# A fused attention and feed-forward kernel: the stretch from y to the gated tiles in a new order

## The chip, the cores and the metric

The kernel runs on one core of one Trainium2 chip. The metric is device time in microseconds (us) of one launch, the median of several runs.

## The reference, cut to what matters

Four batches of 256 tokens of width 128 (float32) go through four blocks, each with a residual. The stretch in question is the end of the first block and the second.

```python
# block 1 (x is normed first; emb = norm(x) + ctx)
y  = sigmoid(q) * num / den                      # AFT attention, then y @ wo + bo
a  = layer_norm(y @ wo + bo + emb) * gamma + beta
ff = relu(a @ w1 + b1) @ w2 + b2                 # 128 -> 512 -> 128
x  = x + (layer_norm(ff + a) * gamma + beta)
# block 2, on norm(x), BitLinear: rows quantised to 8 bits, weights to -1, 0, 1
gate = silu(bitlinear(norm(x), w_gate))          # 128 -> 512
up   = bitlinear(norm(x), w_up)
x    = x + bitlinear(gate * up, w_down)          # rows of gate*up quantised again
# block 3: 16-head attention over ctx (keys, values from ctx, masked), block 4: 8-expert top-1 FFN
```

## The kernel before

All instructions of an engine stand in one list written out by hand; there is no planner. Engines meet at counting semaphores (`sig[...]`), and each list is run strictly in order, so an instruction that waits holds everything behind it. A batch b has two row tiles of 128 tokens (t = 0, 1) and owns two PSUM banks, `bank(b, 0)` and `bank(b, 1)`. Matmuls in near-float32 are made of three float16 passes over high and low parts: ScalarE writes the high part (a rounded copy), VectorE or GpSimd the low part (source minus high).

The stages around the change, for b = 0 to 3 each:

- GpSimd multiplies `th` and `rden` to y (L419); TensorE turns y (L1261 is its transpose helper, L1252 its matmul helper); ScalarE and VectorE write its high and low columns `colsY` (L610, L816); TensorE multiplies by wo.
- Norm LN_A: VectorE takes statistics and moments (L798, L804), GpSimd adds epsilon (L377) and raises to -0.5 (L380) in `rstd_of`, VectorE writes normed rows (L811), TensorE turns them, ScalarE applies gamma and beta (L622, L623), VectorE writes the low part (L816, `n_mem`).
- First layer (TensorE, 4 blocks of 128 hidden columns a batch), relu on ScalarE (L631, high part) and VectorE (L966, low part), second layer on TensorE. A batch order is kept: all four first layers, then all four second layers, with the mask's column counts (L962, and `count_mm`) after the second of these.
- Output norm LN_OUT in pairs of batches: statistics from PSUM, centring with gamma (L980), root on GpSimd, residual into x1 (L987), which adds `xb`, the block's input plus beta, made by GpSimd in eight additions (L431). Then the norm LN_FFN of x1: statistics, root, and on GpSimd the negated mean (L376) and the shift `nmr` (L386); ScalarE writes the rows (L616).
- Row maxima (L1013) and scales (L1006, L1009) on VectorE, one common factor `fac` for all batches (L1020), rounding on ScalarE (L662), turning on TensorE, columns qT on ScalarE (L675).
- Gate and up products for the eight tiles of `GU_ORDER`, (0,0) (1,0) (0,1) (1,1) (2,0) ... (3,1): TensorE, silu on ScalarE (L686), product with up on VectorE (L1033), its maximum (L1027), and per batch a scale again (L1006, L1009). GpSimd (L468) and ScalarE (L679) round the gated tiles for the down product.

Between these stand pieces for later blocks: on GpSimd the low parts of the weights (L392), scaling and rounding of the quantised weights (L425, L438), the low part of the transposed ctx (L441), and after the first `gscale` two clearings (L450, L452) and the residual mask (L457, L462); on ScalarE the high parts (L559), the ctx copy (L627), the column mask (L639 to L643), the value copy `va` (L654) and key copies (L649); on VectorE the small biases `kb16` (L945) and `mbias16` (L949), clipping of the quantised weights (L957) and low parts of keys (L999); on TensorE the projections of values and of half the keys, between the second layers and the turned quantised rows. SP loads everything at the start, except the mask, which waits for the low parts of w1 and w2 and lands in their float32 place.

## Time and profile before

| | us |
|---|---|
| median of 3 runs (lowest, highest) | 248.2 (247.9, 248.48) |
| the profiled execution, its own time | 249.16 |
| its span, first to last instruction | 247.3 |
| busy: TensorE, VectorE, ScalarE, GpSimd | 192.6, 173.2, 135.4, 119.1 |
| mean granted TensorE clock, share of full speed | 0.952 |

The engines are called PE (TensorE; PEld is its weight load), DVE (VectorE), ACT (ScalarE), POOL (GpSimd) and SP. Times are counted from the start of the span. Busy shares are averages over all stages; what bounds a stage is read from the chain of waits and the idle times in it. A row that covers several instructions gives the time from the first's start to the last's end; an instruction's own span overlaps the next one's start by 0.05 to 0.1 us on VectorE and ScalarE, so the distance between two starts is the better price where a queue is full.

### The profile page before, as it was taken

The page shows a single profiled execution, that of the slowest core. Times are in us where ns is not written, and L with a number is a line of the kernel's source. Part 1 is how long each engine was busy: PE and PEld are TensorE (multiplying, and loading weights), DVE is VectorE, ACT ScalarE, POOL GpSimd, SP SyncE. Part 2 cuts the span into 40 slices and gives each one's busy share as a digit, 9 for nine tenths or more (in the row PEclk, how much of TensorE's full clock was granted, in tenths as well). Part 3 has the DMA queues.
Part 4 walks back from the last instruction along what each step waited for, and adds up shares of the span by engine and source line. Part 5 has one row for each costly group of instructions (what it writes and reads, how often), then busy time and mean ns, then how long its engine had stood idle before and what let it go on. Part 6 is the DMA issues. An engine that isn't in the chain of part 4 may idle for free.

```text
span 247.3 us, 4771 instructions
## 1 busy us (share of the span) xinstructions
PE 192.6 (78%) x1750; PEld 134.4 (54%) x1750; DVE 173.2 (70%) x454; ACT 135.4 (55%) x271; POOL 119.1 (48%) x231
## 2 busy tenths in 40 slices
PE   0479865998328479776989988988897895999994
PEld 0358653897203177552433543543555784798883
DVE  4678888994684979869767786886755655739252
ACT  2246744939476578435767567667794256260100
POOL 8131768996649857831587784784221022000000
PEclk9999999999955789998899999999999997999999
DMA  5895040000000000000000000000000000000000
GB/s 169 324 398 219 0 170 4 0 4 0 3 1 0 0 0 3 3 3 3 0 0 5 1 0 3 0 3 0 3 1 3 0 0 4 0 3 21 24 21 21
DMA packets 4461, 8.75 MB, mean 35 GB/s; under 512 B 514, under 2 KB 3026, under 8 KB 4052
## 3 DMA queue, kind: packets, MB, share of 16 engines
q1 hardware_dynamic: 3636, 7.78, 8.4%
q10 hardware_dynamic: 800, 0.63, 0.8%
q8 instruction: 16, 0.26, 0.5%
q14 instruction: 9, 0.07, 0.1%
HBM read 7.89 MB, written 0.52 MB: 34 GB/s over the span
## 4 chain that ended last, share of the span: by engine, by line
PE 31%; POOL 29%; DVE 19%; issue 9%; ACT 7%; DMA 2%; SPq 1%; POOLq 0%; DVEq 0%
PE ps L1252 28%; POOL gate_pt L514 6%; POOL rstd L380 5%; POOL w L400 3%; PE ps L1261 3%; POOL x_in L431 3%; DMA wf<-weights_dram 2%; POOL w L392 2%; POOL vareps L377 2%; DVE gate_pt L1033 2%; DVE mx L1090 2%; DVE amax L1027 2%; DVE stats L798 2%; DVE half_c L1080 2%; ACT gate_pt L758 1%
## 5 line engine op out<-in xcount | busy, mean ns | idle before, releaser
L1090 DVE TENSOR_REDUCE mx<-ps 128x2 f32<-128x512 f32 x64 | 42.2, 686 | 16.6 <-PE ps L1252 16.5
L758 ACT ACTIVATE gate_pt<-ps 128x512 f32<-128x512 f32 x64 | 37.2, 603 | 15.6 <-PE ps L1252 15.3
L1252 PE MATMUL ps<-w,hid_xm 128*128 128x256 f16 (+1 forms) x288 | 30.3, 263 | 0.1
L514 POOL TENSOR_SCALAR gate_pt<-ka_mem 32x256 f16<-32x256 f16 x64 | 25.5, 399 | 4.4
L1252 PE MATMUL ps<-gate_pt,half_c 128*128 128x512 f16 x64 | 25.0, 393 | 3.2 <-issue 1.9
L1252 PEld LDWEIGHTS ps<-w,hid_xm 128*128 128x128 f16 x288 | 25.4, 101 | 3.4 <-issue 0.4
L1252 PE MATMUL ps<-qb,gate_pt 128*128 128x256 f16 x128 | 25.4, 281 | 0.8
L1261 PE MATMUL ps<-cst,rows 128*128 128x128 f32 x32 | 7.5, 333 | 18.0 <-ACT rows L662 8.8
L1252 PE MATMUL ps<-gate_pt,hid_xm 128*32 128x256 f32 x256 | 20.4, 390 | 1.5 <-ACT gate_pt L758 1.5
L1252 PEld LDWEIGHTS ps<-qb,gate_pt 128*128 128x128 f16 x128 | 9.5, 99 | 18.7 <-issue 11.4
L380 POOL TENSOR_TENSOR rstd<-vareps,halfs 128x2 f32<-128x2 f32 x24 | 17.7, 738 | 2.0
L501 POOL TENSOR_SCALAR spread<-mx 128x16 f16<-128x16 f32 x32 | 5.9, 201 | 25.0 <-DVE mx L1090 18.7
L1261 PEld LDWEIGHTS ps<-cst,rows 128*128 128x128 f32 x32 | 3.6, 156 | 22.0 <-ACT rows L662 10.1
L376 POOL TENSOR_SCALAR nmean<-moments 128x2 f32<-128x2 f32 x8 | 2.8, 344 | 24.8 <-DVE moments L804 24.7
L377 POOL TENSOR_SCALAR vareps<-moments 128x2 f32<-128x2 f32 x24 | 6.6, 274 | 12.3 <-DVE moments L804 10.8
L1252 PE MATMUL ps<-brow,esel 128*128 128x128 f16 x56 | 11.3, 225 | 0.0
L1252 PE MATMUL ps<-wf,w 128*128 128x256 f16 x96 | 11.1, 272 | 0.0
L1252 PE MATMUL ps<-stage,w 128*128 128x256 f16 x96 | 11.1, 273 | 0.0
L1252 PEld LDWEIGHTS ps<-gate_pt,half_c 128*128 128x128 f16 x64 | 6.4, 100 | 7.7 <-issue 5.5
L747 ACT ACTIVATE half_b<-ps 128x1024 f16<-128x1024 f32 x8 | 8.3, 1040 | 3.8 <-PE ps L1252 3.8
L1261 PE MATMUL ps<-cst,emb 128*128 128x128 f32 x8 | 2.2, 371 | 10.2 <-DVE emb L850 10.2
L1252 PE MATMUL ps<-ffw,qd_mem 128*128 128x512 f16 x16 | 7.1, 599 | 3.9 <-DVE gate_pt L1033 3.9
(221 smaller groups left out, 505.6 us busy)
## 6 DMA issues: line engine op xcount, KB each, us to landing
stage<-weights_dram SPq DMA_DIRECT2D x2, 1024.0 KB, 11.1
wf<-weights_dram SPq DMA_DIRECT2D x4, 256.0 KB, 8.5
wf<-mask_dram SPq DMA_DIRECT2D x1, 1024.0 KB, 4.8
eb_oT<-ffw_dram SPq DMA_DIRECT2D x1, 768.0 KB, 8.2
ctx_in<-ctx_rows_dram ACTq DMA_DIRECT2D x4, 128.0 KB, 5.9
x_in<-x_dram SPq DMA_DIRECT2D x4, 128.0 KB, 3.1
gate_pt<-ctx_cols_dram SPq DMA_DIRECT2D x1, 512.0 KB, 8.5
out_dram<-ctx_in SPq DMA_DIRECT2D x4, 128.0 KB, 1.7
```

Of the source, the lines that this page charges most:

```text
L377: nc.gpsimd.tensor_scalar(vareps[:, ln, b, :], moments[:, ln, b, :, 1], EPS, 1.0, ALU.add, ALU.mult).then_inc(sig["ln_vareps"], 1)
L380: nc.gpsimd.tensor_tensor(rstd[:, ln, b, :], vareps[:, ln, b, :], halfs[:, 0:TILES], ALU.pow).then_inc(sig["ln_rstd"], 1)
L392: nc.gpsimd.tensor_tensor(w16[:, 1, a:z], wf32(name), w16[:, 0, a:z], ALU.subtract)\
L400: nc.gpsimd.tensor_tensor(w16[:, 1, a:z][:, cols], wf32(name)[:, cols], w16[:, 0, a:z][:, cols], ALU.subtract)\
L431: ins = nc.gpsimd.tensor_tensor(xb[:, b, t], x_in[:, b, t], beta_b[:, :], ALU.add)
L501: ins = nc.gpsimd.tensor_scalar(spread[:, n % 2, t].rearrange("p (g r) -> p g r", g=4)[:, :, 28:32], mx[:, b, 4 * quad:4 * quad + 4, t:t + ...
L514: ins = nc.gpsimd.tensor_scalar(kz[part, n % KRING, k], ka[part, b, quad], 1.0, 0.0, ALU.mult, ALU.add)
L747: nc_act(oh[:, b % 2, 4 * half:4 * half + 4].rearrange("p e n -> p (e n)"), pair(ONEHOT_PAIRS[b]).rearrange("p a n -> p (a n)"), ACT.Copy) ...
L758: nc_act(pt[:, head % PRING].rearrange("p t n -> p (t n)"), ps[:, 2 + head % 2, :], ACT.Exp, scale=DK ** -0.5).then_inc(sig["probs"], 1)
L1090: V.tensor_reduce(mx[:, b, head:head + 2, t], score_bank(4 * n + i).rearrange("p (h n) -> p h n", h=2), AX.X, ALU.max).then_inc(sig["smax" ...
L1252: return nc.tensor.matmul(dst, lhsT, rhs, start=start, stop=stop, skip_group_check=True)
L1261: return nc.tensor.transpose(dst, src, ident)
```

## The change

The same arithmetic is done in another order, and some small operations are merged or moved.

- GpSimd: y of batches 0 and 1 ahead of the low part of wo, the others behind it; the roots of LN_A before the low part of w2; roots of batches 2 and 3 of LN_A in one pair of instructions, those of LN_OUT and LN_FFN in one per two batches; negated mean and shift of LN_FFN gone; wq and wo1 behind the ctx part; the eight additions of beta gone.
- ScalarE: y's high parts ahead of the splits of wk, wv, wq, wo1; ctx copy ahead of LN_A's columns; the split of m1 before the last relu; rows, rounding, keys and gates of batches 2 and 3 follow those of 0 and 1.
- VectorE: one addition of beta over all batches and kb16 ahead of y's low parts; the low parts of the hidden tiles, output norms and mask interleaved; the shift of LN_FFN in one instruction per two batches; scales and factors per two batches; the list is written out.
- TensorE: turning, first and second layers interleaved; half the keys of batches 2 and 3 between gate and up products of batches 0 and 1.

The diff, cut to its core (the other hunks rename counts, or turn loops over b into the functions that the lists call):

```diff
+ROOTS = [(LN_IN, (0,)), (LN_IN, (1,)), (LN_IN, (2,)), (LN_IN, (3,)), (LN_A, (0,)), (LN_A, (1,)), (LN_A, (2, 3)),
+         (LN_OUT, (0, 1)), (LN_FFN, (0, 1)), (LN_OUT, (2, 3)), (LN_FFN, (2, 3)),
+         (LN_ATT, (0,)), (LN_ATT, (1,)), (LN_ATT, (2,)), (LN_ATT, (3,)),
+         (LN_MOE, (0,)), (LN_MOE, (1,)), (LN_MOE, (2,)), (LN_MOE, (3,))]
+
+
+def nth_root(ln, b):
+
+    return 1 + [b in bs and of == ln for of, bs in ROOTS].index(True)
+
+
+def nth_shift(ln, b):
+
+    return b // 2 + 1 if ln == LN_FFN else B // 2 + b + 1
+
+
+MAXIMA = ["row 0", "row 1", "gate 0", "row 2", "gate 1", "row 3", "gate 2", "gate 3", "gate 4", "gate 5", "gate 6", "gate 7"]
+
+
...
-            def rstd_of(ln, b):
-
-                pool.wait_ge(sig["ln_moments"], nth_norm(ln, b))
-                if ln in NMR_TURN:
-                    nc.gpsimd.tensor_scalar(nmean[:, ln, b, :], moments[:, ln, b, :, 0], -1.0, 0.0, ALU.mult, ALU.add)
-                nc.gpsimd.tensor_scalar(vareps[:, ln, b, :], moments[:, ln, b, :, 1], EPS, 1.0, ALU.add,
+            def rstd_of(ln, *bs):
+
+                cols = slice(bs[0], bs[-1] + 1)
+                pool.wait_ge(sig["ln_moments"], nth_norm(ln, bs[-1]))
+                if ln == LN_MOE:
+                    nc.gpsimd.tensor_scalar(nmean[:, ln, bs[0], :], moments[:, ln, bs[0], :, 0], -1.0, 0.0, ALU.mult, ALU.add)
+                nc.gpsimd.tensor_scalar(vareps[:, ln, cols, :], moments[:, ln, cols, :, 1], EPS, 1.0, ALU.add,
                                         ALU.mult).then_inc(sig["ln_vareps"], 1)
-                pool.wait_ge(sig["ln_vareps"], nth_norm(ln, b))
-                nc.gpsimd.tensor_tensor(rstd[:, ln, b, :], vareps[:, ln, b, :], halfs[:, 0:TILES],
-                                        ALU.pow).then_inc(sig["ln_rstd"], 1)
+                pool.wait_ge(sig["ln_vareps"], nth_root(ln, bs[0]))
+                nc.gpsimd.tensor_tensor(rstd[:, ln, cols, :].rearrange("p b t -> p (b t)"),
+                                        vareps[:, ln, cols, :].rearrange("p b t -> p (b t)"),
+                                        halfs[:, 0:len(bs) * TILES], ALU.pow).then_inc(sig["ln_rstd"], 1)
...
+            def gated(b):
+                pool.wait_ge(sig["ysig"], b + 1)
+                nc.gpsimd.tensor_tensor(y[:, b], th[:, b], rden[:, b], ALU.mult).then_inc(sig["y"], 1)
+
+            def ffn_weights_scaled(k):
+                return nc.gpsimd.tensor_scalar(ffw_in[:, k], ffw_in[:, k], wscale[:, k:k + 1], MAGIC, ALU.mult, ALU.add)
+
+            gated(0)
+            gated(1)
             a, z = SEG["wo"]
             pool.wait_ge(sig["w_hi"], 2)
             nc.gpsimd.tensor_tensor(w16[:, 1, a:z], wf32("wo"), w16[:, 0, a:z], ALU.subtract).then_inc(sig["w_lo"], 1)
+            gated(2)
+            gated(3)
             split_lo("w1", 3)
+            rstd_of(LN_A, 0)
+            rstd_of(LN_A, 1)
+            rstd_of(LN_A, 2, 3)
             split_lo("w2", 4)
-
-            for b in range(B):
-                pool.wait_ge(sig["ysig"], b + 1)
-                nc.gpsimd.tensor_tensor(y[:, b], th[:, b], rden[:, b], ALU.mult).then_inc(sig["y"], 1)
-            for b in range(B):
-                rstd_of(LN_A, b)
-
             pool.wait_ge(sig["ffscale"], 1)
             for k in range(3):
-                ins = nc.gpsimd.tensor_scalar(ffw_in[:, k], ffw_in[:, k], wscale[:, k:k + 1], MAGIC, ALU.mult, ALU.add)
+                ins = ffn_weights_scaled(k)
             ins.then_inc(sig["ffw_r"], 1)
-            pool.wait_ge(sig["l_gb"], 32)
-            pool.wait_ge(sig["rows_ready"], nth(R_IN, B - 1))
-            for b in range(B):
-                for t in range(TILES):
-                    ins = nc.gpsimd.tensor_tensor(xb[:, b, t], x_in[:, b, t], beta_b[:, :], ALU.add)
-                ins.then_inc(sig["xb"], 1)
             split_lo("wk", 5)
             split_lo("wv", 6)
-            split_lo("wq", 7)
-            split_lo("wo1", 8)
             pool.wait_ge(sig["ffw_c"], 1)
             nc.gpsimd.tensor_scalar(ffw16[:, :, :].rearrange("p k n -> p (k n)"), ffw_in[:, :, :].rearrange("p k n -> p (k n)"),
                                     -MAGIC, 1.0, ALU.add, ALU.mult).then_inc(sig["ffw_ready"], 1)
             pool.wait_ge(sig["ctxT_hi"], 1)
             nc.gpsimd.tensor_tensor(ctxT[:, 1], ctxT_in, ctxT[:, 0], ALU.subtract).then_inc(sig["ctxT_ready"], 1)
+            split_lo("wq", 7)
+            split_lo("wo1", 8)
             for first in range(0, B, 2):
-                for b in (first, first + 1):
-                    rstd_of(LN_OUT, b)
-                for b in (first, first + 1):
-                    rstd_of(LN_FFN, b)
-                    rows_shift(LN_FFN, b)
+                rstd_of(LN_OUT, first, first + 1)
+                rstd_of(LN_FFN, first, first + 1)
...
-            for name in ("w1", "w2", "wk", "wv", "wq", "wo1"):
-                split_hi(name)
+            split_hi("w1")
+            split_hi("w2")
             for b in range(B):
                 act.wait_ge(sig["turned"], nth(T_Y, b))
                 nc_act(colsY[:, 0, b], bank(b, 1)[:, 0:T], ACT.Copy).then_inc(sig["cols_hi"], 1)
 
+            for name in ("wk", "wv", "wq", "wo1"):
+                split_hi(name)
+            act.wait_ge(sig["l_ctxT"], 16)
+            act.wait_ge(sig["attn_mm"], B)
+            nc_act(ctxT[:, 0], ctxT_in, ACT.Copy).then_inc(sig["ctxT_hi"], 1)
...
+            for b in range(B):
+                if b == B - 1:
+                    split_hi("m1")
                 act.wait_ge(sig["hid_mm"], b + 1)
                 nc_act(hid16[:, 0, b], pair(b), ACT.Relu).then_inc(sig["hid_hi"], 1)
...
+            ffn_rows(0)
+            ffn_rows(1)
             for b in range(B):
                 act.wait_ge(sig["vproj"], b + 1)
                 for t in range(TILES):
                     ins = nc_act(va[:, b, t, :, 0:DK],
                                  bank(b, 1)[:, t * D:(t + 1) * D].rearrange("p (h k) -> p h k", h=NH), ACT.Copy)
                 ins.then_inc(sig["va_ready"], 1)
-
-            def round_rows(b):
-
-                act.wait_ge(sig["ascale"], nth(0, b))
-                for t in range(TILES):
-                    ins = nc_act(rows[:, b, t], rows[:, b, t], ACT.Copy, scale=amax[:, b, 1, t:t + 1], bias=MAGIC)
-                ins.then_inc(sig["q1"], 1)
-
-            for b in range(B):
-                act_rows(LN_FFN, b, lambda t: x1[:, b, t])
-                if b == B - 1:
-                    round_rows(0)
-                    round_rows(1)
-                key_hi(b, 0)
+            round_rows(0)
+            round_rows(1)
+            key_hi(0, 0)
+            key_hi(1, 0)
+            quantised_columns(0)
+            quantised_columns(1)
+            gate(0)
+            gate(1)
+            ffn_rows(2)
+            ffn_rows(3)
+            key_hi(2, 0)
+            gate(2)
+            key_hi(3, 0)
+            gate(3)
             round_rows(2)
             round_rows(3)
-            for b in range(B):
-                act.wait_ge(sig["turned"], nth(T_QUANT, b))
-                nc_act(qT[:, b], bank(b, 0)[:, 0:T], ACT.Copy, bias=-MAGIC).then_inc(sig["q1T_ready"], 1)
-
-            def round_gated(b):
-                act.wait_ge(sig["ascale"], nth(1, b))
-                nc_act(g[:, b, 1], g[:, b, 1], ACT.Copy, scale=amax[:, b, 3, 1:2], bias=MAGIC).then_inc(sig["q2_act"], 1)
-
-            for u, (b, t) in enumerate(GU_ORDER):
-                act.wait_ge(sig["gu_mm"], u + 1)
-                act.wait_ge(sig["gscale"], 1)
-                if t:
-                    act.wait_ge(sig["g"], u - 1)
-                nc_act(silu[:, b], bank(b, 0), ACT.Silu, scale=fac[:, b, 0, t:t + 1]).then_inc(sig["silu"], 1)
-                if (b, t) in ((2, 1), (3, 1)):
-
-                    round_gated(b - 2)
+            quantised_columns(2)
+            quantised_columns(3)
+            gate(4)
+            gate(5)
+            gate(6)
+            round_gated(0)
+            gate(7)
+            round_gated(1)
...
+            dve.wait_ge(sig["l_gb"], 32)
+            dve.wait_ge(sig["rows_ready"], nth(R_IN, B - 1))
+            V.tensor_tensor(xb[:, :, :, :].rearrange("p b t n -> p (b t) n"), x_in[:, :, :, :].rearrange("p b t n -> p (b t) n"),
+                            beta_b[:, :].unsqueeze(1).to_broadcast([P, B * TILES, D]), ALU.add).then_inc(sig["xb"], 1)
+            dve.wait_ge(sig["mbias_hi"], 1)
+            V.scalar_tensor_tensor(kb16[0:2, :], kb_h[:, :], c("lo_2", 2), kb_in[:, :], ALU.mult, ALU.add)\
+                .then_inc(sig["mbias_ready"], 1)
...
+            def ffn_shift(first):
+                two = slice(first, first + 2)
+                dve.wait_ge(sig["ln_rstd"], nth_root(LN_FFN, first))
+                V.scalar_tensor_tensor(nmr[:, LN_FFN, two, :], moments[:, LN_FFN, two, :, 0], -1.0, rstd[:, LN_FFN, two, :],
+                                       ALU.mult, ALU.mult).then_inc(sig["ln_nmr"], 1)
...
+            def row_scales(first):
+                two = slice(first, first + 2)
+                quant_scale(two, 0, nth_max("row", first + 1))
+                V.tensor_tensor(fac[:, two, 0:2, :], amax[:, two, 0:1, :].to_broadcast([P, 2, 2, TILES]),
+                                mean[:, 0:2].unsqueeze(1).unsqueeze(3).to_broadcast([P, 2, 2, TILES]), ALU.mult)\
+                    .then_inc(sig["gscale"], 1)
...
+            hidden_lo(0)
+            dve.wait_ge(sig["mbias_hi"], 2)
+            dve.wait_ge(sig["cols_zero"], 2)
+            V.scalar_tensor_tensor(mbias16[0:2 * NE, 0:EH + D], mbias_h[:, :], c("lo_16", 2 * NE), mbias_in[:, :], ALU.mult, ALU.add)\
+                .then_inc(sig["mbias_ready"], 1)
+            hidden_lo(1)
+            dve.wait_ge(sig["y"], B)
+            dve.wait_ge(sig["l_mask"], 16)
+            V.tensor_scalar(ind[:, :, :, :].rearrange("p a t n -> p (a t n)"), mask_in.rearrange("p a t n -> p (a t n)"),
+                            0.0, None, ALU.is_equal).then_inc(sig["mask_ind"], 1)
+            hidden_lo(2)
+            out_stats(0)
+            out_centred(0)
+            hidden_lo(3)
+            out_stats(1)
+            out_centred(1)
+            dve.wait_ge(sig["mbias_ready"], 2)
+            for j in range(2):
+                V.tensor_scalar(out_bias[0:2 * NE, j * D:(j + 1) * D], mbias16[0:2 * NE, EH:EH + D],
+                                c("parity")[0:2 * NE, j:j + 1], None, ALU.mult).then_inc(sig["mbias_ready"], 1)
+            residual(0)
+            residual(1)
+            ffn_stats(0)
+            out_stats(2)
+            out_stats(3)
+            ffn_shift(0)
+            out_centred(2)
+            out_centred(3)
+            residual(2)
+            residual(3)
+            row_max(0)
+            row_max(1)
+            row_scales(0)
+            ffn_stats(2)
+            key_lo(0, 0)
+            key_lo(1, 0)
+            ffn_shift(2)
+            gate_up(0)
+            gate_up(1)
+            gate_max(0)
+            row_max(2)
+            gate_up(2)
+            gate_max(1)
+            row_max(3)
+            row_scales(2)
+            key_lo(2, 0)
+            gate_up(3)
+            gate_max(2)
+            key_lo(3, 0)
+            gate_max(3)
+            gate_scale(0)
+            gate_scale(1)
+            gate_up(4)
+            gate_up(5)
+            gate_max(4)
+            gate_up(6)
+            gate_max(5)
+            gate_up(7)
+            gate_max(6)
+            gate_max(7)
+            gate_scale(2)
+            gate_scale(3)
...
+            normed_turned(0)
+            normed_turned(1)
+            normed_turned(2)
+            pe.wait_ge(sig["w_lo_pool"], 1)
+            first_layer(0)
+            normed_turned(3)
+            first_layer(1)
+            first_layer(2)
+            pe.wait_ge(sig["w_lo_pool"], 2)
+            second_layer(0)
+            first_layer(3)
+            second_layer(1)
+            pe.wait_ge(sig["mask_ind"], 1)
+            for a in range(B):
+                for t in range(TILES):
+                    ins = mm(bank(a // 2, 1)[:, (a % 2) * T:(a % 2 + 1) * T], ones16[:, 0:P], ind[:, a, t], t == 0,
+                             t == TILES - 1)
+            ins.then_inc(sig["count_mm"], 1)
+            second_layer(2)
+            second_layer(3)
...
+            keys_first_half(0)
+            keys_first_half(1)
+            quantised_turned(0)
+            quantised_turned(1)
+            pe.wait_ge(sig["ffw_ready"], 1)
+            gate_up(0)
+            gate_up(1)
+            keys_first_half(2)
+            gate_up(2)
+            keys_first_half(3)
+            gate_up(3)
+            quantised_turned(2)
+            quantised_turned(3)
+            gate_up(4)
+            gate_up(5)
+            gate_up(6)
+            gate_up(7)
...
```

## Rows read from the trace of the kernel before

**Rows 1.** The chain of waits, 30 to 60 us: start, length (us), engine, tile, line.

```profile
41.53 2.66 POOL eb_oT L425 x3
...
44.19 6.44 POOL x_in L431 x8
...
55.08 2.10 POOL y_mem L441
```

**Rows 2.** The waits, 26 to 110 us: who for whom, total us, times, longest.

```profile
ACT rows L616 <- POOL nmr L386: 5.7, 4, 4.0
...
DVE emb L987 <- POOL rstd L380: 5.6, 4, 2.8
```

**Rows 3.** The timeline of VectorE, gate stretch: start, length (us), then the instructions.

```profile
77.19 1.53 DVE L1033 SCALAR_TENSOR_TENSOR gate_pt<-gate_pt,fac,ps 128x512 f32<-128x512 f32 x2 [2.73 <-ACT gate_pt L686]
...
80.45 0.68 DVE L1027 TENSOR_REDUCE amax<-gate_pt 128x1 f32<-128x512 f32 x1
...
81.05 0.74 DVE L1033 SCALAR_TENSOR_TENSOR gate_pt<-gate_pt,fac,ps 128x512 f32<-128x512 f32 x1
...
89.57 0.17 DVE L1009 RECIPROCAL amax<-amax 128x2 f32<-128x2 f32 x1
```

**Rows 4.** The timeline of GpSimd: y, two roots, the mask additions.

```profile
32.37 2.77 POOL L419 TENSOR_TENSOR y<-th,rden 128x256 f32<-128x256 f32 x4
...
37.56 0.70 POOL L380 TENSOR_TENSOR rstd<-vareps,halfs 128x2 f32<-128x2 f32 x1
...
38.62 0.70 POOL L380 TENSOR_TENSOR rstd<-vareps,halfs 128x2 f32<-128x2 f32 x1
...
79.89 4.48 POOL L462 TENSOR_TENSOR wf<-wf,colsA 128x512 bf16<-128x512 bf16 x4
```

**Rows 5.** Instructions grouped by line and shape, GpSimd: count | busy us, mean ns.

```profile
L485 POOL TENSOR_TENSOR wnorm<-wnorm,minus_ones 128x8 f32<-128x8 f32 x1 | 1.7, 1657 | 0.1
```

**Rows 6.** The same view, VectorE: a product with two inputs in SBUF.

```profile
L893 DVE TENSOR_TENSOR y_mem<-y_mem,cst 128x512 f32<-128x512 f32 x1 | 0.7, 692 | 0.1
```

**Rows 7.** The timeline of VectorE: quotient, statistics, kb16, relu, residual, a scale.

```profile
33.78 0.36 DVE L877 SCALAR_TENSOR_TENSOR th<-th,ps 128x256 f32<-128x256 f32 x1
...
36.43 0.49 DVE L798 BATCH_NORM_STATS2 stats<-ps 128x6 f32<-128x128 f32 x2
...
44.46 0.94 DVE L945 SCALAR_TENSOR_TENSOR kb<-kb_h,cst,kb_in 2x512 f16<-2x512 f16 x1
...
48.59 4.60 DVE L966 SCALAR_TENSOR_TENSOR hid_xm<-ps,hid_xm 128x1024 f16<-128x1024 f32 x4
...
58.35 0.61 DVE L987 SCALAR_TENSOR_TENSOR emb<-ctx_in,rstd,x_in 128x128 f32<-128x128 f32 x2 [2.81 <-POOL rstd L380]
...
83.55 0.85 DVE L1006 TENSOR_SCALAR amax<-amax 128x2 f32<-128x2 f32 x1
```

**Rows 8.** Line L431 at 46.4 and 48.9 us: ns min/median/max, first and last start.

```profile
L431 POOL TENSOR_TENSOR x_in<-x_in,beta_b x1: 2566/2566/2566, 46.4 to 46.4; 128x128 f32<-128x128 f32 x1
...
L431 POOL TENSOR_TENSOR x_in<-x_in,beta_b x3: 450/451/452, 48.9 to 49.8; 128x128 f32<-128x128 f32 x3
```

**Rows 9.** The timeline of TensorE: two blocks of the first layer.

```profile
42.67 0.49 PE L1252 MATMUL ps<-n_mem,w 128*128 128x256 f16 x3
...
43.10 0.49 PE L1252 MATMUL ps<-n_mem,w 128*128 128x256 f16 x3
```

**Rows 10.** The timeline of ScalarE: rows, rounding, a silu.

```profile
62.58 0.88 ACT L616 ACTIVATE rows<-emb,nmr,rstd 128x128 f32<-128x128 f32 x2 [1.25 <-POOL nmr L386]
...
71.86 1.26 ACT L662 ACTIVATE rows<-rows,amax 128x128 f32<-128x128 f32 x4
...
76.40 0.69 ACT L686 ACTIVATE gate_pt<-ps,fac 128x512 f32<-128x512 f32 x1 [0.47 <-PE ps L1252]
```

**Rows 11.** Busy time and granted clock of TensorE in one stretch (us, count, clock).

```profile
68.00:80.00 12.00, 6.25 (x17) 0.50 0.00 1
```

**Rows 12.** DMA issues: size, median us from issue to landing.

```profile
wf<-mask_dram SPq DMA_DIRECT2D x1, 1024.0 KB, 4.8
```

More of the change, by code:

```diff
@@ L1358, in _, with normed_turned @@
                 ins.then_inc(sig["attn_mm"], 1)
-            for b in range(B):
+            def normed_turned(b):
                 pe.wait_ge(sig["rows_ready"], nth(R_A, b))
@@ L1371, in _, with second_layer @@
                 ins.then_inc(sig["hid_mm"], 1)
[L1372 to L1373 removed]
+            def second_layer(b):
                 pe.wait_ge(sig["hid_ready"], b + 1)
```

163 lines of the change are left out of this document (72 added, 91 removed).

## The prediction, before the change was run

> **What bounds the kernel now.** I read the chain of waits first, cut to the stretch from the gated y tiles (32 us) to the last scale of the gated tiles (89.7 us). From 41.5 to 59 us the chain is GpSimd's instruction list: scaling the quantised weights (2.66 us), beta additions (6.44), four weight splits, a rounding, the ctx split (2.10), and only then the roots of the output norm [rows 1]. The waits say who stands behind it: VectorE waits 5.6 us in the residual (L987) for GpSimd's roots, and ScalarE waits 5.7 us in L616 for the shifts, with TensorE behind it [rows 2]. From 77.2 us on VectorE sets the pace: eight gate products, 0.65 us apart from what follows, and eight maxima, 0.60, then scales until 89.7 us [rows 3]. Behind that point the diff changes no order, only names of counts and one form (the root of a single batch stays 128x2). So the question is how much earlier than 89.7 us the last scale (L1009) ends; the rest follows it.
>
> **GpSimd's part.** The eight beta additions go (6.44 us here), as do the four mean negations and four shifts of LN_FFN. Of LN_A's four roots the last two become one, and LN_OUT and LN_FFN take one per two batches: a root of one batch repeats every 38.62 - 37.56 = 1.06 us, of which 0.70 is the power [rows 4]. For 128x4 the trace has no power. 128x2 costs 0.70 and 128x8 costs 1.66 [rows 4, 5]: on that line 128x4 is 0.70 + 2 x 0.16 = 1.02 us, bounds 0.70 and 1.66. I take 1.02. A root of two batches is then 0.27 + 1.02 = 1.3 us instead of 2.1. What the first batch of a pair sees grows from 1.0 to 1.3, what the second sees shrinks by 0.8.
>
> **VectorE's part.** It gains one 128x1024 addition with both inputs in SBUF. The nearest row is 128x512 with two SBUF inputs, 0.69 us [rows 6]: not less than that, not more than twice it, 1.38. I take 1.2, near the upper end since most of such an instruction grows with its columns, and 1.15 until the next may start. Moved ahead of the low parts of y is kb16 as well (512 columns, two SBUF inputs): 0.69 by [rows 6], 0.94 where it stands beside GpSimd's additions [rows 7]; I take the lower, 0.65 until the next starts. Four maxima's scales (8 small instructions of 0.1 to 0.2) become 4, one more factor and two shifts come in: about zero.
>
> **The shared path of the two.** One beta addition on GpSimd took 2.57 us beside VectorE's clipping and mask, where others took 0.45 [rows 8]; VectorE's 128x2 scale took 0.85 us at 83.55 instead of 0.16, beside GpSimd's mask additions, four in 4.48 us [rows 4, 7]. So each can hold the other for a whole instruction or more. The Trainium skill (SBUF — State Buffer, Who interferes with whom) says that a VectorE instruction with two SBUF inputs, or in a two-port mode, and a GpSimd instruction that reads SBUF exclude one another for a whole instruction, while a PSUM source with one SBUF input is free. Both rows agree. The rule speaks against moving beta. Taken the other way, with no exclusion, the gain would be 5.1 instead of 3.2 us (case A).
>
> **Walk through the new order**, with this trace's times as the clock.
> 1. VectorE ends the last quotient at 34.1 [rows 7]. GpSimd has y(0) to y(2) by 32.6, since y now stands ahead of the 2.27 us of splits (before, y(0) began at 32.37 [rows 4]). The addition holds VectorE to 35.2 and with it GpSimd's y(3), which is ready at 34.15; kb16 to 35.85; y(3) 35.85 to 36.55. TensorE turns all four y before it multiplies, so attention's output starts at 36.9 and VectorE's LN_A statistics at 37.8 instead of 36.43 [rows 7]. This step costs 1.4 us. The statistics end at 40.5, the three roots at 42.1, the normed rows at 43.45.
> 2. First layer of batch 0 starts at 43.85 (42.67 before [rows 9]). Each batch takes four such pieces of 0.43 to 0.44, 1.75 us; I take 1.7 for a second layer (27 matmuls of half the columns a tile). Turning batch 3 now stands behind first layer 0, so VectorE idles about 2.5 us until its low part at 47.35, then clips (0.9) and starts hidden_lo(0) at 48.25, 48.59 before [rows 7]. TensorE: second layer 0 at 49.45, first layer 3 to 52.9, second layer 1 to 54.6, the counts to 55.5.
> 3. VectorE then works without a gap: hidden_lo 1.15 each, mbias 0.7, mask 1.15 plus 0.6 held by GpSimd's 2.1 us ctx split, statistics 0.65, centring 0.55. Statistics of batch 1 end at 57.15 (before, VectorE waited 2.81 us here for GpSimd [rows 7]); GpSimd is free (ctx split to 51.9, wq and wo1 to 53.4), the pair's root is there at 58.65, where the first residual began at 58.35 [rows 7]; residuals end at 59.8, statistics of x1 at 60.85. So pair 0 gains nothing up to here.
> 4. Here pair 1 is already in: its second layers end at 58.9, its output statistics run at 60.85 to 62.2 while GpSimd takes the root of pair 0 (60.95 to 62.25). ScalarE's rows(0) start at 62.5 (62.58 before [rows 10]), rows(1) end 64.1; residuals of pair 1 end at 64.75; maxima and scales of pair 0 at 65.8, where the old order computed its one factor for all four batches only after the last row maximum.
> 5. ScalarE copies va (estimated 1.4 for eight tiles), rounds rows 0 and 1 (0.6 each [rows 10]), takes key_hi 0 and 1 (0.5 each) and the columns; key_lo(0) on VectorE, of the shape of a product, ends at 68.1; TensorE starts gate_up(0) at 68.3, the silu follows at 69.3 and takes 0.7 [rows 10], product g(0) starts at 70.05. Before, g(0) began at 77.19 [rows 3]. That is 7.1 us earlier, with less of the other work done.
> 6. From g(0) VectorE has 8 x (0.65 + 0.60) = 10.0 us of products and maxima, row maxima of pair 1 0.6, its scales 0.5, key_lo(2), (3) 1.3, gate scales 1.0: 13.4. Waits: 0.2 for silu(1); 1.2 for silu(2), which stands on ScalarE behind rows(2), (3) and key_hi(2) and on TensorE behind keys(2); 1.0 for small scales held by GpSimd's mask additions, four of 1.12 that now run about 73.5 to 78; 0.7 for silu(6) and silu(7), which has round_gated(0) ahead of it. Sum 16.5: the last scale ends at 70.05 + 16.45 = 86.5 us, against 89.65. The gain is 3.15, say 3.2 us.
>
> **What hides what.** The mask's load now waits for the w2 split on GpSimd, at 43.2 instead of 32.4; it is needed at 51.25 and takes 4.8 us to land [rows 12], so 3 us are left; if they were gone, the whole VectorE queue behind the mask would wait for it. SP queues nothing but the output behind it. ScalarE's four splits of wk to wo1 and the ctx copy move behind y, about 1.5 and 1.0 us, into its wait for the turned rows (37.4 to 41.6): free. Without that cover 1.0 would stand ahead of A(0). GpSimd's clearing of va, the mask and its four additions start after the roots of pair 1 (68.2) and end at 78; needed is q2(0) at 80.5. Behind the last scale the path is unchanged.
>
> **The sum.** The profiled execution took 249.16 us, its span 247.3. Minus 3.2: 245.96 and a span of 244.1. It lies 0.96 above the median of the runs shown, 248.2; the median of the changed kernel is then 245.0.
>
> **Rivals.**
> A, the locks hardly bite: y(3) is not held, kb16 takes 0.6, the scales are not delayed. Then steps 1 to 4 shift by about 1.3 more, minus the 0.4 absorbed by TensorE in step 2, and step 6 by 1.0: gain 5.1, time 243.1. For it: the four y took 2.77 us, undisturbed, with VectorE's quotient from PSUM beside them [rows 4]. Against it: [rows 8].
> B, TensorE's clock and ScalarE's order bound the gate. TensorE's keys are two pieces like those of [rows 9] a batch, 0.88 us at 2.4 GHz; while TensorE idled the granted clock fell to 0.50, that is 1.2 GHz, and stood there from 68 to 80 us [rows 11]. Now keys(2), (3) stand between gate_up(1), (2) and (3): at half clock 0.88 more each, 1.75 in all, and nothing of it covered if silu(2) and silu(3) are what VectorE waits for: gain 3.2 - 1.75 = 1.4, time 246.8. For it: TensorE is idle from 61.5 to 64.5 in the new order too. Against: VectorE has work queued for most of that stretch.
> C, slower. The place is the shared path of VectorE and GpSimd; the price is one GpSimd instruction, 1.15 us, for each further hold on the path. Open to it beyond what I count are the low part of A(3) against the wk split, a residual and the shift of pair 1 against a root, and the factor of pair 1 against a mask addition: four, 4 x 1.15 = 4.6 us. 4.6 - 3.2 = 1.4 slower, 249.6 us; it decides from the third hold on (3.45 us). For it: 2.57 in place of 0.45 [rows 8]. Against: VectorE's waits for roots say that GpSimd is done or idle when residual and shift run, and of eight scales only one took 0.85.
> That the change does not do what it says, paired roots costing as two: 0.8 us at two places, inside the forecast's range.
>
> **Chances.** Forecast 0.45 (its own range 243.9 to 246.1), A 0.25, B 0.20, C 0.07, nothing measurable 0.03. What a measurement of this kernel can tell from no change is 0.2%, 0.5 us. Faster: 0.45 + 0.25 + nearly all of B = 0.88; same 0.04; slower 0.08. The range takes A's far side, 5.9 us of gain, and B's: 242.3 to 247.2.
>
> **What would show it.** Right: statistics of LN_A (L798 of before) about 1.4 us later; no wait of VectorE's residual for a root above 1 us; the first silu near 69 us; the last gate scale near 86.5; everything behind it the same length (157.6 us from there to the end). Wrong: y(3) not held beside the beta addition (A); granted clock 0.5 with silu(2) or silu(3) waiting for TensorE, and VectorE idle over 2.5 us in the gate stretch (B); several VectorE scales of 0.5 us and more (C); a different length behind the last scale, for which I have no mechanism.

## The result and the profile after

| | before | after | forecast |
|---|---|---|---|
| median of 18 runs each (lowest, highest), us | 248.31 (246.55, 250.08) | 250.69 (248.72, 252.1) | 245.0 |
| span of the profiled execution | 247.3 | 249.5 | 244.1 |
| first LN_A statistics | 36.43 | 38.20 | 37.8 |
| hidden_lo(0) | 48.59 | 51.61 | 48.25 |
| first residual | 58.35 | 62.60 | 58.7 |
| first product g(0) | 77.19 | 74.01 | 70.05 |
| last gate scale, end | 89.74 | 91.08 | 86.5 |

The ratio is 1.0083, interval 1.0056 to 1.0111: slower by 2.1 us (2.4 between the medians), where 3.2 less were forecast. Ratios, here and below, leave out runs more than 1.5% above the fastest of their kernel (none of the change, three of e1's twelve); medians keep them. The profile shows the loss in three places. First VectorE's timeline from y to the residual (start, length, idle time ahead of it), to be laid beside [rows 7]:

```profile
33.91 1.21 DVE L986 TENSOR_TENSOR x_in<-x_in,beta_b 128x1024 f32<-128x1024 f32 x1
35.03 1.21 DVE L989 SCALAR_TENSOR_TENSOR kb<-kb_h,cst,kb_in 2x512 f16<-2x512 f16 x1
...
38.20 0.49 DVE L851 BATCH_NORM_STATS2 stats<-ps 128x6 f32<-128x128 f32 x2 [0.63 <-PE ps L1363]
...
39.48 0.49 DVE L851 BATCH_NORM_STATS2 stats<-ps 128x6 f32<-128x128 f32 x2 [0.50 <-PE ps L1363]
...
50.40 0.42 DVE L869 TENSOR_TENSOR n_mem<-n_mem 128x256 f16<-128x256 f32 x1 [3.00 <-ACT n_mem L658]
...
51.61 1.22 DVE L1012 SCALAR_TENSOR_TENSOR hid_xm<-ps,hid_xm 128x1024 f16<-128x1024 f32 x1
...
62.60 1.14 DVE L1033 SCALAR_TENSOR_TENSOR emb<-ctx_in,rstd,x_in 128x128 f32<-128x128 f32 x4 [0.47 <-POOL rstd L410]
```

GpSimd's timeline beside it (y(3), the split behind it, the first root of two batches), for [rows 4]:

```profile
34.07 1.63 POOL L444 TENSOR_TENSOR y<-th,rden 128x256 f32<-128x256 f32 x1 [1.55 <-DVE th L930]
35.66 1.60 POOL L423 TENSOR_TENSOR w<-wf,w 128x512 f16<-128x512 f32 x1
...
43.09 1.01 POOL L410 TENSOR_TENSOR rstd<-vareps,halfs 128x4 f32<-128x4 f32 x1
```

TensorE's turning of y(3), and its windows (us, busy, count, granted clock, then DMA share and GB/s):

```profile
35.76 0.69 PE L1372 MATMUL ps<-cst,y 128*128 128x128 f32 x2 [2.75 <-POOL y L444]
```
```profile
32.00:34.00 2.00, 0.69 (x5) 1.00 0.00 0
34.00:36.00 2.00, 0.24 (x1) 0.71 0.00 0
36.00:38.00 2.00, 1.72 (x15) 0.50 0.00 0
38.00:40.00 2.00, 2.00 (x22) 0.50 0.04 8
40.00:42.00 2.00, 1.90 (x19) 0.58 0.00 0
...
44.00:46.00 2.00, 1.04 (x5) 0.77 0.00 0
```

Its timeline in the first layer of batch 0, first piece, and the turning of batch 3 behind the last, for [rows 9]:

```profile
45.97 0.80 PE L1363 MATMUL ps<-n_mem,w 128*128 128x256 f16 x3 [0.48 <-DVE n_mem L869]
46.56 0.42 PE L1363 MATMUL ps<-esel,brow 128*128 128x256 f16 x1
...
48.93 0.38 PE L1372 MATMUL ps<-cst,rows 128*128 128x128 f32 x2
49.15 0.49 PE L1363 MATMUL ps<-n_mem,w 128*128 128x256 f16 x3
```

In the kernel before, every window from 30 to 46 us was at 1.00. Now the beta addition (L986) begins when the last quotient is out; y(3) takes 1.63 us instead of the 0.72 that it takes in e1, and kb16, which starts its record at 35.03, takes 1.21. TensorE stands still for 2.75 us, its clock falls to 0.50 (1.2 GHz), and attention's output, which waited for y(3) only by the order of its list, is multiplied at half speed: statistics of the four batches come 1.28 us apart where 0.67 was VectorE's own pace. At 44 us the clock was down again (0.77), and the first layer of batch 0 took 2.96 us (45.97 to 48.93) instead of 1.75; the first three of its four pieces of three matmuls show 0.80 to 0.84, the fourth 0.50, those of batch 1 0.49. Batch 3's rows are turned behind it, and VectorE waits 3.00 us for them, to 50.40.

The gate stretch, VectorE, for [rows 3]:

```profile
74.01 1.41 DVE L1081 SCALAR_TENSOR_TENSOR gate_pt<-gate_pt,fac,ps 128x512 f32<-128x512 f32 x2 [0.84 <-ACT gate_pt L709]
...
78.96 1.00 DVE L1065 TENSOR_SCALAR amax<-amax 128x4 f32<-128x4 f32 x1
...
80.09 0.97 DVE L1073 TENSOR_TENSOR fac<-amax,mean 128x8 f32<-128x8 f32 x1
...
90.91 0.17 DVE L1068 RECIPROCAL amax<-amax 128x2 f32<-128x2 f32 x1
```

Scale and factor of batches 2 and 3 took 1.97 us together, where free of holds they take 0.17 and 0.14 (in e6, below); they ran beside GpSimd's mask (77.67 to 82.15).

### The profile page after: what moved, and what is told of

Read it like the earlier page. It is cut to its first block, busy times and chain, and to the rows that moved or that the text cites. A ratio compares the mean times of both kernels' runs of the same rounds, so it can differ in the third digit from the quotient of the medians.

```text
span 249.5 us, 4753 instructions
## 1 busy us (share of the span) xinstructions
PE 199.2 (80%) x1750; PEld 139.1 (56%) x1750; DVE 177.0 (71%) x454; ACT 135.2 (54%) x271; POOL 111.0 (45%) x205
## 4 chain that ended last, share of the span: by engine, by line
PE 24%; POOL 16%; DVE 7%; issue 7%; ACT 4%; POOLq 0%; DVEq 0%
PE ps L1363 23%; POOL gate_pt L543 9%; POOL w L431 3%; DVE mx L1201 2%; ACT gate_pt L811 2%; POOL spread L530 1%; POOL rstd L410 1%; PE ps L1372 1%; DVE half_c L1191 1%; DVE stage L1265 1%; POOL wnorm L514 1%; ACT rows L651 1%; POOL vareps L407 1%; DVE ka_mem L1299 0%; ACT eb_oT L758 0%
## 5 line engine op out<-in xcount | busy, mean ns | idle before, releaser
L410 POOL TENSOR_TENSOR rstd<-vareps,halfs 128x2 f32<-128x2 f32 (+1 forms) x19 | 15.8, 831 | 1.6
L407 POOL TENSOR_SCALAR vareps<-moments 128x2 f32<-128x2 f32 (+1 forms) x19 | 5.7, 298 | 22.3 <-DVE moments L857 21.5
L1372 PEld LDWEIGHTS ps<-cst,rows 128*128 128x128 f32 x32 | 4.0, 163 | 16.9 <-DVE rows L864 5.1
L1363 PE MATMUL ps<-brow,esel 128*128 128x128 f16 x56 | 12.1, 241 | 0.0
L406 POOL TENSOR_SCALAR nmean<-moments 128x2 f32<-128x2 f32 x4 | 2.0, 500 | 21.2 <-DVE moments L857 21.2
L1363 PE MATMUL ps<-colsA,w 128*128 128x256 f16 x60 | 11.0, 307 | 0.2 <-DVE colsA L869 0.2
L1363 PE MATMUL ps<-y_mem,w 128*128 128x256 f16 x48 | 8.3, 298 | 3.0 <-ACT hid_xm L716 3.0
L1363 PE MATMUL ps<-w,y_mem 128*128 128x128 f16 x72 | 8.3, 250 | 2.9 <-DVE y_mem L869 1.8
```

Of the source, the lines that this page charges most:

```text
L407: nc.gpsimd.tensor_scalar(vareps[:, ln, cols, :], moments[:, ln, cols, :, 1], EPS, 1.0, ALU.add, ALU.mult).then_inc(sig["ln_vareps"], 1)
L410: nc.gpsimd.tensor_tensor(rstd[:, ln, cols, :].rearrange("p b t -> p (b t)"), vareps[:, ln, cols, :].rearrange("p b t -> p (b t)"), halfs[ ...
L1363: return nc.tensor.matmul(dst, lhsT, rhs, start=start, stop=stop, skip_group_check=True)
L1372: return nc.tensor.transpose(dst, src, ident)
```

## The experiments

Each ran against the kernel before on the same chip, in five rounds. Ratios are to that kernel. e1 to e4 shared one chip, e5 to e8 a second, e9 to e11 a third, e12 and e13 a fourth, and the kernel before had medians of 247.79 to 248.31 us there; so across these groups the ratio is the better measure (0.001 is 0.25 us), and differences below are given by medians first, by ratios behind.

| | median us | ratio (interval) |
|---|---|---|
| the change | 250.69 | 1.0083 (1.0056, 1.0111) |
| e1 beta and kb16 late | 246.54 | 0.9924 (0.9889, 0.9958) |
| e2 fillers | 248.33 | 1.0017 (0.9982, 1.0052) |
| e3 before, beta early | 247.97 | 0.9988 (0.9951, 1.0025) |
| e4 batch 3 turned first | 248.10 | 0.9988 (0.9954, 1.0021) |
| e5 = e1 + e4 | 245.52 | 0.9896 (0.9856, 0.9937) |
| e6 = e5, mask late | 245.58 | 0.9906 (0.9871, 0.9941) |
| e7 beta on GpSimd, kb16 late | 247.61 | 0.9991 (0.9962, 1.0020) |
| e8 only beta late | 248.86 | 0.9997 (0.9961, 1.0033) |
| e9 = e5, mask ahead of clearings | 249.66 | 1.0038 (1.0003, 1.0072) |
| e10 = e9 + fillers at y | 248.46 | 1.0016 (0.9984, 1.0048) |
| e11 = e10 + fillers in the gate | 248.53 | 1.0018 (0.9988, 1.0048) |
| e12 = e5, clearings in waits | 245.45 | 0.9874 (0.9827, 0.9922) |
| e13 = e12 + fillers at y | 246.13 | 0.9911 (0.9883, 0.9939) |

**e1**, the two instructions moved in VectorE's list:

```diff
             quotient(3)
-            (beta addition into xb, kb16)
 ...
             for b in range(B):
+                if b == B - 1:
+                    (beta addition into xb, kb16)
                 dve.wait_ge(sig["cols_hi"], nth(C_A, b))
```

> The changed kernel with VectorE's beta addition and kb16 moved from ahead of y's low parts into its 3.0 us wait for batch 3 of LN_A. Theory 1 (the addition and kb16 on the path, the held y(3) and TensorE's clock that fell meanwhile are the loss): y(3) takes 0.7 us instead of 1.63, LN_A's statistics begin near 36.2 instead of 38.2, granted clock 1.0 from 36 to 42, the last gate scale 3 to 4 us earlier than 91.1, time 3 us or more below the changed kernel, below the kernel before. Theory 2 (the loss is made in the gate stretch by its own waits): last gate scale within 1.5 us of 91.1.

4.2 us below the change (3.9 by the ratios) and 0.8% below the kernel before. GpSimd and VectorE of e1:

```profile
34.07 0.72 POOL L444 TENSOR_TENSOR y<-th,rden 128x256 f32<-128x256 f32 x1 [1.55 <-DVE th L930]
```
```profile
36.07 0.49 DVE L851 BATCH_NORM_STATS2 stats<-ps 128x6 f32<-128x128 f32 x2
...
87.39 0.17 DVE L1068 RECIPROCAL amax<-amax 128x2 f32<-128x2 f32 x1
```

y(3) at the same time as in the change, in 0.72 us; clock 1.00 from 34 to 38; the last scale 3.5 us earlier, while the stretch from g(0) to it is 16.5 us, against 16.9 in the change. The two profiled spans differ by 4.8 us (249.5 and 244.7): 3.1 lie ahead of g(0), 0.4 in the gate stretch, 1.3 behind the last scale. So most of it comes from the head, not from the gate.

TensorE's windows of e1 and, under it, of e2 (the next experiment):

```profile
34.00:36.00 2.00, 1.16 (x18) 1.00 0.00 0
36.00:38.00 2.00, 1.96 (x36) 1.00 0.03 8
```
```profile
34.00:36.00 2.00, 1.66 (x16) 1.00 0.00 0
36.00:38.00 2.00, 1.47 (x22) 1.00 0.00 0
38.00:40.00 2.00, 1.77 (x32) 1.00 0.04 8
```

**e2**, the clock alone; the hold stays:

```diff
             for b in range(B):                      # turning y
+                if b == B - 1:
+                    pe.wait_ge(sig["ysig"], 1)
+                    for _ in range(22):
+                        mm(bank(0, 0)[:, T:2 * T], ones16[:, 0:P], ones16[:, :], True, True)
                 pe.wait_ge(sig["y"], b + 1)
```

> The changed kernel with 22 extra matmuls of 256 columns on TensorE, whose result nobody reads, between turning y(2) and y(3), where it idled 2.75 us. If the low clock (0.50 to 0.58 from 36 to 42 us) is a cost of its own: granted clock 1.0 there, statistics of LN_A 0.67 apart instead of 1.28, last moments of LN_A about 1.9 us earlier, time 1.5 to 2 us below the changed kernel. If only the held y(3) counts: same time as the changed kernel, within 0.5 us.

y(3) still takes 1.63 us (GpSimd's timeline of e2, below), the clock is 1.00 from 34 to 42, VectorE waits for no statistics, and the last scale begins at 89.13, 1.8 us earlier. The time falls 2.4 us by the medians, 1.6 by the ratios (intervals just apart, 1.0056 and 1.0052), for 22 matmuls whose result nobody reads.

```profile
34.28 1.63 POOL L444 TENSOR_TENSOR y<-th,rden 128x256 f32<-128x256 f32 x1 [1.55 <-DVE th L930]
```

So of what e1 takes back the clock is about half: 1.8 of 3.5 us at the last scale, 2.4 of 4.2 by medians, 1.6 of 3.9 by ratios. The hold, kb16 and the addition are the rest.

How long TensorE waits does not settle by itself whether the clock falls. With y(3) unheld it waits 1.83 or 1.84 us in the profiles of e1, e5, e6, e7, e9 and e12; from 34 to 38 us the granted clock was 1.00 in e1, e7 and e9, but 0.58, 0.80 and 0.61 in e5, e6 and e12. With waits of 2.27 us (e8) and 2.75 us (the change, e4) it fell each time. TensorE's turning of y(3) and its window in e1 and, under it, in e5, whose lists up to here are the same:

```profile
34.84 0.44 PE L1372 MATMUL ps<-cst,y 128*128 128x128 f32 x2 [1.83 <-POOL y L444]
34.00:38.00 4.00, 3.12 (x50) 1.00 0.01 4
```
```profile
34.54 0.64 PE L1372 MATMUL ps<-cst,y 128*128 128x128 f32 x2 [1.83 <-POOL y L444]
34.00:38.00 4.00, 3.46 (x31) 0.58 0.00 0
```

**e3**, the beta edit alone in the kernel before:

```diff
-            (GpSimd: eight beta additions, ahead of the split of wk)
 ...         (VectorE, behind the last quotient)
+            (one beta addition into xb, kb16)
```

> The kernel before with one edit: beta's addition as one VectorE instruction, with kb16, ahead of y's low parts; GpSimd's eight additions gone. If that edit carries the loss: LN_A's statistics 1.5 to 3 us later than 36.4 and a low clock there; the 6.4 us taken off GpSimd give back 2 to 4 us at 58 us, so the time is about that of before, 247 to 249. If moving beta is harmless: 244 to 246.

First statistics at 38.42 (2 us late), the clock at 0.69 from 36 to 38 and 0.50 to 40 where it was 1.00; the first residual at 58.59 all the same, for GpSimd is free earlier. What the edit takes at the head it gives back at the root: no difference in time is seen.

**e4**, TensorE's list:

```diff
             normed_turned(2)
+            normed_turned(3)
             pe.wait_ge(sig["w_lo_pool"], 1)
             first_layer(0)
-            normed_turned(3)
```

> The changed kernel with batch 3 of LN_A turned before the first layer of batch 0, as in the kernel before. VectorE waited 3.0 us for ScalarE's columns of batch 3. If that wait is on the path: clipping and hidden_lo(0) 2 us earlier than 50.7 and 51.6, time 1 to 2 us below the changed kernel. If TensorE's first layers bound there anyway: second layer 0 moves by under 0.5 us, same time.

VectorE of e4 at the point where the change had its wait:

```profile
46.87 1.91 DVE L1007 TENSOR_SCALAR eb_oT<-eb_oT 128x1536 f32<-128x1536 f32 x1
48.70 1.21 DVE L1012 SCALAR_TENSOR_TENSOR hid_xm<-ps,hid_xm 128x1024 f16<-128x1024 f32 x1
```

The wait of 3.0 us is gone, hidden_lo(0) at 48.70, last scale at 88.16. The wait was on the path: 2.6 us by medians, 2.4 by ratios. The profile can't be read for the whole of it, since e4's last moments of LN_A began at 41.17, 1.3 us before those of the change (42.47), ahead of the place of the edit: the quotient was 0.3 us earlier, and the clock rose sooner (0.69 against 0.50 from 38 to 40). Of the 2.9 us at hidden_lo(0) 1.6 are left for the edit, and in these TensorE's first layer ran at 1.00.

**e5 to e8.** e5 makes the edits of e1 and e4 both. The others, shortened:

```diff
             pool.wait_ge(sig["colmask"], 1)            # e6: e5, and
+            pool.wait_ge(sig["gscale"], 2)
 ...                                                    # e7: the change, and on GpSimd
             ins.then_inc(sig["ffw_r"], 1)
+            (eight beta additions, as before)
             split_lo("wk", 5)
 ...                                                    # e7 on VectorE: beta addition out, kb16 moved
 ...                                                    # as in e1; e8: beta addition moved as in e1,
 ...                                                    # kb16 stays behind the last quotient
```

> The changed kernel with two edits together: beta's addition and kb16 in front of batch 3's low part of LN_A (alone: 246.54 us), and batch 3 turned ahead of the first layer of batch 0 (alone: 248.10). If both take different microseconds, last gate scale near 85.5 and about 244.5 us. If the wait for batch 3 was what hid the moved addition and kb16 (2.3 us), they now stand on VectorE's path: 246 to 247 us, no better than the first edit alone.

1.0 us below e1 (0.7 by the ratios), 2.6 below e4 (2.3). The intervals of e1 and e5 overlap, so the gain over e1 is not shown; that the late addition fills the wait which the other turn removes would explain it, and was not tried by itself.

> The same two edits, and GpSimd starts the residual mask (L486, L491) only after the row scales of batches 2 and 3 (gscale at 2). In the changed kernel VectorE's scale took 1.00 and its factor 0.97 us beside that mask. If the shared path is what held them: both back to 0.15 to 0.2, gate stretch (first product to last scale) 1.6 us shorter than 16.5, time 1 to 1.6 us below the run without this edit. If the mask then holds the gate scales of batches 0 and 1 and rounding on GpSimd instead: no gain, within 0.5 us.

VectorE of e6:

```profile
75.98 0.17 DVE L1066 TENSOR_SCALAR amax<-amax 128x4 f32<-128x4 f32 x1
...
76.28 0.14 DVE L1074 TENSOR_TENSOR fac<-amax,mean 128x8 f32<-128x8 f32 x1
...
79.50 0.58 DVE L1066 TENSOR_SCALAR amax<-amax 128x2 f32<-128x2 f32 x1
...
80.19 0.99 DVE L1066 TENSOR_SCALAR amax<-amax 128x2 f32<-128x2 f32 x1
```

Scale and factor are free, the gate scales of batches 0 and 1 are held instead, 0.58 and 0.99 where the change has 0.15 each: the hold went where the mask went.

> The changed kernel with beta back on GpSimd as eight additions behind the scaled weights, and kb16 in VectorE's wait for batch 3. If moving beta to VectorE is what the gain needs, the additions (3.6 to 6.4 us) push GpSimd's ctx split and the first root past their due times: 1 to 3 us above 246.54. If GpSimd has the room in the new order (it idled 2.3 us at 49.5 and 3.0 us at 58.2): within 0.5 us of 246.54.

0.7% above e1 (1.7 us; 1.1 by medians), intervals just apart (from 0.9962, to 0.9958), and not to be told from the kernel before. The profiles of both have the same last scale (87.46, 87.39), but e7's profiled run, 246.61 us, was the second fastest of its twelve, so it can't show the difference; where it comes from stays open.

> The changed kernel with only beta's addition moved to VectorE's wait for batch 3; kb16 stays ahead of y's low parts. If the addition holds y(3) and kb16 does not: y(3) 0.7 us, statistics of LN_A near 36.8, 1 us behind the run with both moved, full clock, about 247 us. If kb16 holds y(3) in the same way (both have two SBUF inputs): y(3) 1.5 us or more, a low clock, 248 us or more.

Between the two answers: kb16 (0.73 us) is enough to make y(3) 1.15 us instead of 0.72, and the clock was 0.61 and 0.54 from 36 to 40. The time is 2.3 us above e1 (1.8 by the ratios), intervals just apart (0.9961, 0.9958). Leaving out one at 251.75, its runs fall into two groups, five from 246.1 to 247.5 us and six from 248.8 to 249.4; the profiled one is of the second, so that the clock fell in it need not hold for the first.

**e9 to e11**, the order on GpSimd (mask L486 and L491, then the clearings), then 14 fillers at y, then 8 more each ahead of `quantised_turned(2)` and `gate_up(6)`:

```diff
-            (memset of spread, of va and of its ones column)   # e9: e5, on GpSimd
             (mask: L486, then the four additions of L491)
+            (the same three memsets)
 ...                                                            # e10: e9, on TensorE
+                    for _ in range(14): (filler of e2)
 ...                                                            # e11: e10, and at both places
+            for _ in range(8): (filler)
```

> The changed kernel with the two edits of e5 (245.52 us) and, on GpSimd, the residual mask (L486, L491) ahead of the clearings of spread and va instead of behind them, so that it ends near 75.7 us and the clearings, which read nothing, lie beside VectorE's scales. If reading instructions of GpSimd hold VectorE's small scales: scale and factor of batches 2 and 3 take 0.15 to 0.2 us instead of 1.0 each, and no gate scale is held either, last gate scale 1 to 1.6 us earlier than 87.5, about 244.3 us. If clearings hold them as well, or ScalarE's and TensorE's own chain bounds batches 2 and 3: within 0.5 us of 245.5.

A miss, and the most telling one: 4.1 us slower than e5 (3.5 by the ratios). VectorE and GpSimd of e9:

```profile
75.66 2.93 DVE L1065 TENSOR_SCALAR amax<-amax 128x4 f32<-128x4 f32 x1
```
```profile
75.44 0.53 POOL L489 MEMSET spread<- 128x512 f16 x1
75.91 2.66 POOL L491 MEMSET hid_xm<- 128x3072 f32 x1
```

A scale of 128x4 elements waited for a clearing that reads nothing, to its end at 78.57. The gate stretch grew to 18.0 us, 1.3 more than in e5 and 1.5 more than in e1, and last scale to first down product took 4.2 us against 3.7 in e5 (3.2 before). That is 1.9 us of the 2.3 between the two profiled spans (248.0 and 245.7); e5's profiled run was the slowest of its six, so the profiles show less than the medians, and the rest stays open.

> The same and 14 extra matmuls of 256 columns on TensorE between turning y(2) and y(3), their result unread. In e5, e6 and e8 the granted clock fell to 0.58 to 0.80 between 34 and 38 us though y(3) was not held long, in e1 and e7 it did not. If that is chance from run to run and costs up to 2 us: clock 1.0 from 34 to 42, LN_A's statistics 0.67 apart, median 0.5 to 1.5 us below e9 and the runs closer together. If not: within 0.5 us.

1.2 us below e9 (0.5 by the ratios), intervals overlap, and the runs lie no closer together; clock 1.00 from 34 to 38 and 0.98 to 42. A gain is not shown.

> The same and 8 extra matmuls each before turning the quantised rows of batch 2 and before gate_up(6). TensorE ran at 0.50 from 78 to 90 us, and the turning of the gated tiles, 32 transposes, took 6.2 us in the changed kernel where it took about 2 us for 16 at full clock. If the clock costs there: granted clock up between 78 and 92, last scale to first down product (L1168) 3.2 us or less instead of 3.6 to 3.8, 0.5 to 1 us below e10. If the fillers at the low clock only lengthen TensorE's list: equal or up to 1 us slower.

The clock rose (0.72, 0.86, 1.00 for 78 to 90, against 0.50, 0.50, 0.54) and last scale to first down product fell from 4.05 to 3.2 us, but the median is that of e10. A gain from that clock is not shown.

**e12, e13**, the clearing of va in halves:

```diff
+            rstd_of(LN_OUT, 0, 1)
+            pool.wait_ge(sig["ff_mm"], B)
+            nc.gpsimd.memset(va[:, 0:2, :, :, DK:32], 0.0)
+            rstd_of(LN_FFN, 0, 1)
+            rstd_of(LN_OUT, 2, 3)
+            nc.gpsimd.memset(va[:, 2:4, :, :, DK:32], 0.0)
 ...         (ones column, rstd_of(LN_FFN, 2, 3), then spread and the mask)
```

> The changed kernel with the two edits of e5 (245.52 us) and GpSimd's clearing of va (2.66 us) cut into halves that stand in its waits between the roots, the ones column behind the second; the mask then starts at 69.5 and ends near 76. If GpSimd's long instructions are what holds VectorE's scales (2.93 us beside the clearing in e9): scale of batches 2 and 3 held by 0.4 us at most, none of the gate scales, gate stretch 15.2 us or less instead of 16.7, time 244 to 245 us. If not: 245.5.

> The same and the 14 extra matmuls between turning y(2) and y(3). If the clock's fall around 36 us is chance from run to run and costs: median 0.5 to 1 us below e12 and a narrower spread. If not: within 0.5 us of e12.

VectorE of e13:

```profile
70.09 1.39 DVE L1083 SCALAR_TENSOR_TENSOR gate_pt<-gate_pt,fac,ps 128x512 f32<-128x512 f32 x2
...
84.99 0.17 DVE L1070 RECIPROCAL amax<-amax 128x2 f32<-128x2 f32 x1
```

GpSimd of e13:

```profile
58.90 1.38 POOL L476 MEMSET hid_xm<- 128x1536 f32 x1 [1.58 <-PE ps L1365]
60.34 0.20 POOL L407 TENSOR_SCALAR vareps<-moments 128x4 f32<-128x4 f32 x1
```

The stretch is 14.9 us in place of 16.5 in e1 and 16.9 in the change: with no scale held it is 2.0 us shorter, where the forecast had 1.0 for the holds. Part of that only moved: the shift of batches 2 and 3 (L1049), just ahead of g(0), took 1.70 us beside GpSimd's mask (68.26 to 70.15) where it took 0.15 in the change. From the first low part of a key (key_lo, L1055; L1053 in the change), ahead of that shift, to the last scale it is 17.8 us against 19.2, so 1.4 us are gained. And the first half waits for the last second layer (58.90) and pushes the root of batches 0 and 1 behind it (60.34), and the median of e12 is that of e5. The fillers of e13 held the clock at 1.00 from 34 to 38, where e12's profile, of its slowest run, has 0.61, and gave nothing on top (246.13 against 245.45 us, intervals overlap). e5 and e12 are the best versions: 1.0 and 1.3% below the kernel before, both about 2% under the change.

## Why the prediction was wrong

Taken by its steps, times of the change against those of the forecast:

- **Step 1 failed, by a term that it put at nothing: TensorE's clock.** The hold of y(3) and of kb16 was there, in the other order (y(3) before kb16). kb16 took 1.21 us, where I had taken the lower of two rows, 0.69, without a reason; VectorE's y low parts began at 36.17, forecast 35.85. Attention's output even started on time, at 36.72, forecast 36.9. But the clock fell around TensorE's wait of 2.75 us, which followed from my own times for y(2) and y(3), and I had priced the multiplications behind it at 2.4 GHz: the statistics ended at 42.72, forecast 40.5, and what I priced at 1.4 us was 1.8 at the first statistics and 3.5 at the last moments. In e2, at full clock, they ended at 40.59. I named the clock only as rival B in the gate. e2 shows what that term is worth: 2.4 us by medians, 1.6 by ratios.
- **Step 2 failed with it.** Forecast hidden_lo(0) at 48.25, measured 51.61. Of the 3.4 us 2.1 come from step 1, the rest from the first layer at the low clock, ahead of batch 3's turn. VectorE's wait for that turn is not what the forecast missed: the walk counted it at 2.5 us, it was 3.0. What I did not ask is whether the order is worth having; e4 says that without it the change is 2.4 to 2.6 us faster.
- **Steps 3 to 5 were near.** From hidden_lo(0) to g(0) I gave 21.8 us, it took 22.4; from rows(0) to g(0) 7.55, it took 7.6. A root of two batches takes 1.01 us for its power, forecast 1.02; the beta addition 1.21, forecast 1.2.
- **Step 6 was near.** 16.45 us forecast, 17.1 measured, the difference in scale and factor (1.7 held, 1.0 counted).
- **The tail was not constant.** 158.4 us behind the last scale instead of 157.6. From 90 to 94 us the granted clock was 0.50 and 0.78, from 102 to 106 0.64; in the kernel before it was 1.00 in these stretches. The fifteen profiles sort by the second fall: in the nine where the clock fell between 96 and 106 us the time behind the last scale was 158.0 to 159.0 us, in the six where it stayed at 1.00 it was 156.5 to 157.6. So what I took as a constant differs with that fall by some 1 us.
- Sum: 3.95 us at g(0), 0.6 in the gate, 0.8 in the tail make the 5.4 between the spans 244.1 and 249.5.

Rival C had the right sign and 0.07: it named the shared path, but priced only held instructions. Rival B named the clock and looked for it in the wrong stretch. The true case joins them: a hold on one engine becomes a wait of TensorE, and the clock falls at it. The range ended at 247.2 since no case of mine multiplied its delay.

Shown are: the place of the two instructions (e1), the clock as a cost of its own (e2; its interval is only just apart, and the fillers of e10 and e13, where y(3) was not held, showed no gain), batch 3's turn (e4), the holds in the gate (e6, e9, e13). Not shown: why the clock falls in one execution and not in another at the same wait, and why it fell in the tail. Open: e7 against e1, and what is left between e9 and e5.

## What to carry to other kernels

Price a wait of TensorE twice, once for its length and once for what runs behind it at half the clock (a term that may or may not come: at 1.83 us it came in three profiles of six), and look at the granted clock in windows of 2 us where you lengthen an idle time. An instruction that "fills a gap" on VectorE can hold GpSimd, and GpSimd's long clearings and masks hold even a 4-column VectorE scale (0.17 us becomes 2.93 and 1.00); place them by what stands beside them on the other engine's list. Move work into an engine's measured wait (e1), not ahead of the first instruction of the next stage.
